# The front state's turn between its two gate steps: VectorE block transposes and sixteen on-chip transfers instead of eight TensorE transposes, with the loop in another order

## The reference, cut to what matters

```
layer 0, three steps:  a  = adj @ h                        (per graph)
                       z  = sigmoid(a.W3 + h.U3 + b)       r = sigmoid(a.W4 + h.U3 + b)
                       hv = tanh(a.W5 + (r*h).U5 + b)      h = (1-z)*h + z*hv
layer 1: q,k,v from x;  rel = adj.T * (q @ k.T), each row divided by its norm;  rel @ v
layer 2: (adj @ x) @ W + b          layer 3: (normalised adj) @ (x @ W) + b
```

## Time and profile before

| | |
|---|---|
| median of three runs | 1271.95 us |
| the profiled execution | 1271.8 us |
| its span, first to last instruction | 1270.0 us |
| mean granted TensorE clock | 0.995 of full |
| TensorE busy / VectorE / ScalarE / GpSimd | 98% / 81% / 46% / 15% |
| one turn of the loop | 76.5 us |

### The profile page before, as it was taken

One profiled execution on the slowest core, in us unless ns is written; L12 is line 12 of the kernel. 1 busy time (PEld: TensorE's weight loads), 2 busy tenths in 40 slices (PEclk: granted clock), 3 DMA queues, 4 the chain that ended last, 5 costly groups with the idle time before them and its releaser, 6 DMA issues.

```text
span 1270.0 us, 21112 instructions
## 1 busy us (share of the span) xinstructions
PE 1240.6 (98%) x7664; PEld 1103.3 (87%) x7664; DVE 1031.4 (81%) x2274; ACT 583.7 (46%) x1007; POOL 192.4 (15%) x366
## 2 busy tenths in 40 slices
PE   7799999999999999999999999999999999999996
PEld 6589899898988989899898988989889898998895
DVE  5668889788888878888788888878888788895898
ACT  4444444444444444454444444444454445444442
POOL 0001112020210202112020110202112021110023
PEclk9999999999999999999999999999999999999999
DMA  7020110202001020010202002020010202000000
GB/s 199 1 50 1 38 30 1 66 0 59 7 17 50 0 66 0 33 33 0 66 0 50 17 17 50 0 66 0 21 45 0 66 0 49 17 17 18 1 1 34
DMA packets 86168, 37.56 MB, mean 30 GB/s; under 512 B 64768, under 2 KB 83200, under 8 KB 86144
## 3 DMA queue, kind: packets, MB, share of 16 engines
q1 hardware_dynamic: 84592, 36.71, 10.6%
q0 software_dynamic: 192, 0.52, 0.2%
q10 hardware_dynamic: 1360, 0.01, 0.1%
HBM read 20.45 MB, written 8.39 MB: 23 GB/s over the span
## 4 chain that ended last, share of the span: by engine, by line
PE 94%; DVE 4%; DMA 1%; POOL 1%; issue 0%; ACT 0%; ACTq 0%; DVEq 0%
PE b_ps L430 46%; PE f_ps L430 43%; PE f_ps L525 2%; PE b_ps L525 1%; DMA bias_in<-in_L_gnn_u_b 1%; PE b_ps L571 1%; DVE f_stats L1251 0%; DVE hf_feat L1267 0%; DVE normed L1267 0%; POOL f_rstd L364 0%; DVE f_cand L1184 0%; DVE b_stats L1251 0%; DVE f_kept L1178 0%; ACTq L827 0%; DVE f_a_lo L1162 0%
## 5 line engine op out<-in xcount | busy, mean ns | idle before, releaser
L362 POOL TENSOR_TENSOR b_var_eps<-b_moments,eps 128x2 f32<-128x2 f32 x120 | 44.1, 368 | 827.6 <-DVE b_moments L1258 827.6
L364 POOL TENSOR_TENSOR b_rstd<-b_var_eps,neg_half 128x2 f32<-128x2 f32 x120 | 97.0, 808 | 9.4
L866 ACT ACTIVATE f_z<-f_ps,bias_z 128x512 f32<-128x512 f32 x66 | 45.2, 685 | 92.5 <-PE f_ps L430 92.5
L870 ACT ACTIVATE f_cand<-f_ps,bias_c 128x512 f32<-128x512 f32 x66 | 45.5, 690 | 85.1 <-PE f_ps L430 85.1
L1168 DVE TENSOR_TENSOR f_gate<-f_gate,hf_feat 128x512 f32<-128x512 f32 x66 | 45.2, 685 | 46.2 <-ACT f_gate L858 46.0
L1251 DVE BATCH_NORM_STATS2 b_stats<-b_ps 128x6 f32<-128x256 f32 x180 | 68.3, 421 | 13.9 <-PE b_ps L430 13.3
L430 PE MATMUL f_ps<-adjT_hi,hf_node_hi 128*128 128x256 f32 x264 | 74.6, 283 | 0.0
L430 PE MATMUL f_ps<-adjT_hi,hf_node_lo 128*128 128x256 f32 x264 | 74.3, 282 | 0.0
L430 PE MATMUL f_ps<-adjT_lo,hf_node_hi 128*128 128x256 f32 x264 | 74.2, 281 | 0.0
L1290 DVE TENSOR_TENSOR b_rh_lo<-b_ps,b_rh_hi 128x512 fp32r<-128x512 f32 x90 | 61.9, 688 | 13.7 <-ACT b_rh_hi L824 13.4
L824 ACT ACTIVATE f_a_hi<-f_ps 128x512 fp32r<-128x512 f32 x66 | 39.0, 593 | 71.8 <-PE f_ps L430 71.8
(11 more groups left out here) (325 smaller groups left out, 4610.5 us busy)
## 6 DMA issues: line engine op xcount, KB each, us to landing
x_front<-in_x SPq DMA_DIRECT2D x16, 512.0 KB, 3.5
x_blocks<-in_x SPq DMA_DIRECT2D x60, 128.0 KB, 3.4
input_t<-hf_feat SPq DMA_DIRECT2D x15, 512.0 KB, 2.9
out<-result SPq DMA_DIRECT2D x15, 512.0 KB, 3.0
b_cand<-in_L_gnn_u_w SPq DMA_DIRECT2D x2, 256.0 KB, 8.9
bias_out<-in_L_gnn_bias POOLq DMA_DIRECT2D x4, 128.0 KB, 6.3
b_z<-in_L_gnn_w_w SPq DMA_DIRECT2D x1, 512.0 KB, 11.4
b_gate<-in_L_gnn_w_w SPq DMA_DIRECT2D x1, 512.0 KB, 12.4
```

The costliest lines, as they stand in the source:

```text
L364: pool.tensor_tensor(Y.rstd[:, g], Y.var_eps[:, g], neg_half[:], ALU.pow).then_inc(Y.s_rstd, 1)
L866: act.activation(L.z[:, k], L.ps0[:, k], ACT.Sigmoid, bias=bias_z[:, k:k + 1]).then_inc(L.s_z, 1)
L870: act.activation(L.cand[:, k], L.ps1[:, k], ACT.Tanh, bias=bias_c[:, k:k + 1]).then_inc(L.s_tanh, 1)
```

## The change

Only the turn of the front state inside the 14 bodies is done in another way; the prologue, the `finish` part and the back state keep `turn_h`. Two VectorE block transposes (`turn_state`) write each 32x32 block, turned in itself, to `blocks`, which lies over `front.gate`. SyncE then sends sixteen transfers of 32 partitions by 256 elements (32 KB each), which put the blocks on their right partitions in `moved`, over `front.z`. ScalarE and VectorE make `node_hi` and `node_lo` from there (`moved_hi`, `moved_lo`), once all sixteen have landed.

```diff
+        state_f.blocks, state_f.moved = quarters(front.gate), quarters(front.z)
 (SyncE)
+            def move_blocks(S, turn):
+                sp.wait_ge(S.s_blocks, 2 * turn)
+                for a in range(4):
+                    for b in range(4):
+                        sp.dma_start(S.moved[32 * a:32 * a + 32, b],
+                                     S.blocks[32 * b:32 * b + 32, a]).then_inc(S.s_moved, 16)
                 keep_input(p)
+                move_blocks(state_f, p)
                 store(main, p - 1)
 (ScalarE)
+            def moved_hi(S, v, g, turn):
+                act.wait_ge(S.s_moved, 256 * turn)
+                ...
+                rows = S.moved[:, :, g * P:(g + 1) * P].rearrange("p q (u i) -> p u q i", i=32)
+                copy(S.node_hi[:, g].rearrange("p h (c q i) -> p (h c) q i", q=4, i=32), rows).then_inc(S.s_node_hi, 1)
 (VectorE)
+            def turn_state(S, v, c):
+                dve.wait_ge(S.s_feat, upto(v, c))
+                out = S.blocks.rearrange("p q (u c i) -> p u q c i", c=C, i=32)[:, :, :, c]
+                dve.transpose(out, S.feat[:, c].rearrange("p (u q i) -> p u q i", q=4, i=32)).then_inc(S.s_blocks, 1)
+            def moved_lo(S, v, g):
+                dve.wait_ge(S.s_node_hi, upto(v, g))
+                ...
+                dve.tensor_tensor(cells(S.node_lo), rows, full(cells(S.node_hi)), ALU.subtract).then_inc(S.s_node_lo, 1)
```

All hand-written orders change with it. TensorE's body, in its middle part, is now:

```diff
                 candidate_reset(front, 2 * p, 1)
+                for k in range(2):
+                    keys(main, q, k)
                 values(main, q, 0)
+                relate(main, q, 0)
+                values(main, q, 1)
                 relate(main, q, 1)
-                for k in range(2):
-                    turn_h(state_f, 2 * p + 1, k)
-                values(main, q, 1)
+                base(front, 2 * p + 1, 0)
                 sum_squares(main, q, 0)
                 attend(main, q, 0)
-                mix(front, 2 * p + 1, 0)
+                base(front, 2 * p + 1, 1)
+                for k in range(2):
+                    mix(front, 2 * p + 1, k)
                 sum_squares(main, q, 1)
                 attend(main, q, 1)
-                mix(front, 2 * p + 1, 1)
-                for k in range(2):
-                    base(front, 2 * p + 1, k)
                 reset(front, 2 * p + 1, 0)
```

More of the change, by code:

```diff
@@ L686, in finish @@
                     turn_h(state_f, 2 * LAST + 1, k)
-                candidate_mixed(back, LAST - 1, 0)
-                update(back, LAST - 1, 0)
+                for k in range(2):
+                    update(back, LAST - 1, k)
                 for k in range(2):
@@ L706, in finish @@
                 candidate_reset(back, LAST - 1, 1)
-                base(front, 2 * LAST + 2, 0)
                 for k in range(2):
                     mix(front, 2 * LAST + 2, k)
+                base(front, 2 * LAST + 2, 0)
+                turn_sum(main, LAST - 1, 0)
+                reset(front, 2 * LAST + 2, 0)
+                keys(main, LAST - 1, 0)
                 base(front, 2 * LAST + 2, 1)
[L711 to L714, removed]
+                reset(front, 2 * LAST + 2, 1)
                 update(front, 2 * LAST + 2, 0)
+                turn_sum(main, LAST - 1, 1)
+                update(front, 2 * LAST + 2, 1)
+                relate(main, LAST - 1, 0)
                 candidate_mixed(front, 2 * LAST + 2, 0)
-                update(front, 2 * LAST + 2, 1)
-                keys(main, LAST - 1, 0)
                 candidate_reset(front, 2 * LAST + 2, 0)
@@ L928, in body @@
+                sum_hi(main, q, 1)
                 for k in range(2):
[L929 to L939, removed]
@@ L940, in body @@
-                update_gate(front, 2 * p, 0)
-                rh_hi(front, 2 * p, 1)
+                    rh_hi(front, 2 * p, k)
+                for k in range(2):
+                    update_gate(front, 2 * p, k)
+                for k in range(2):
+                    candidate(front, 2 * p, k)
                 keys_hi(main, q, 0)
-                candidate(front, 2 * p, 0)
+                feat_hi(state_f, 2 * p + 1, 0)
+                keys_hi(main, q, 1)
+                values_hi(main, q, 0)
@@ L953, in body @@
                 relation_hi(main, q, 1)
+                for k in range(2):
+                    moved_hi(state_f, 2 * p + 1, k, p)
                 relation_squares(main, q, 1)
-                values_hi(main, q, 1)
-                feat_hi(state_f, 2 * p + 1, 1)
                 for k in range(2):
                     a_hi(front, 2 * p + 1, k)
-                for k in range(2):
-                    conv_x_hi(main, q, 0, k)
+                conv_x_hi(main, q, 0, 0)
+                reset_gate(front, 2 * p + 1, 0)
@@ L1026, in finish @@
-                for k in range(2):
-                    sum_hi(main, LAST - 1, k)
-                for k in range(2):
-                    reset_gate(front, 2 * LAST + 2, k)
+                feat_hi(state_f, 2 * LAST + 2, 0)
+                node_hi(state_f, 2 * LAST + 2, 0, 5)
+                candidate(back, LAST - 1, 0)
+                node_hi(state_f, 2 * LAST + 2, 1, 6)
+                feat_hi(state_f, 2 * LAST + 2, 1)
+                candidate(back, LAST - 1, 1)
+                a_hi(front, 2 * LAST + 2, 0)
@@ L1030, in finish @@
+                sum_hi(main, LAST - 1, 0)
+                a_hi(front, 2 * LAST + 2, 1)
+                sum_hi(main, LAST - 1, 1)
+                reset_gate(front, 2 * LAST + 2, 0)
+                keys_hi(main, LAST - 1, 0)
+                rh_hi(front, 2 * LAST + 2, 0)
+                reset_gate(front, 2 * LAST + 2, 1)
                 update_gate(front, 2 * LAST + 2, 0)
-                for k in range(2):
-                    rh_hi(front, 2 * LAST + 2, k)
+                rh_hi(front, 2 * LAST + 2, 1)
@@ L1042, in finish @@
[L1042 to L1050 removed]
+                sum_hi(last_pair, 0, 0)
+                values_hi(main, LAST - 1, 0)
@@ L1343, in body @@
+                rh_lo(back, q, 0)
+                reset_h(back, q, 1)
                 turn_blocks(p, 1)
+                a_lo(front, 2 * p, 0)
+                rh_lo(back, q, 1)
                 keep(back, q, 1)
+                input_lo(p, 1)
+                a_lo(front, 2 * p, 1)
+                residual(main, back, q, q, 1)
                 candidate_part(back, q, 0)
-                input_lo(p, 1)
                 new_sum(main, q, q, 0)
-                for k in range(2):
-                    a_lo(front, 2 * p, k)
@@ L1370, in body @@
+                normalise(main, q, 0, 0)
+                keep(front, 2 * p, 1)
+                moments_of(main, q, 0, 1)
+                sum_lo(main, q, 1)
+                candidate_part(front, 2 * p, 0)
+                first_h(p, 0)
+                turn_state(state_f, 2 * p + 1, 0)
+                candidate_part(front, 2 * p, 1)
+                first_h(p, 1)
+                turn_state(state_f, 2 * p + 1, 1)
+                keys_lo(main, q, 0)
                 normalise(main, q, 0, 1)
```

468 lines of the change are left out of this document (227 added, 241 removed).

## The result

The changed kernel takes 1329.71 us (median of 4 runs), the kernel before 1272.86 us beside it: a ratio of 1.044 [1.042, 1.046]. So it is slower, as forecast, but by 57 us and not by 17, and 5 us beyond the upper end of the range. The profiled execution took 1329.41 us, its span is 1327.3 us. One of the four runs took 1349.07 us, at a mean clock of 0.961 where the other three had 0.982 to 0.985; there is no trace of it.

A forecast was written before the change was run, and what follows sets the result against it. TensorE, never waiting in the 14 bodies, was taken as the bound. Each body waits 2.1 us and saves 0.87: 14 x (2.1 - 0.87) = +17.2 us on 1271.8, so 1289.0; range 1262 to 1325.

The forecast's parts named there:

- step 3: Sixteen sends in SyncE's one queue: 0.54 us from one start to the next, the last starting at T+11.5.
- the new order: Changed order of engine work at the start of the loop body and on GpSimd: costed at nothing.
- Removed turn: Front state's transposes on TensorE taken out of 14 loop bodies: 0.87 us a body, 12.2 us gained in all.
- Steps 1 and 2: New front state on ScalarE and VectorE done at T+2.43, then its second block transpose done at T+3.3.
- T: Moment in a loop body at which TensorE goes on from candidate_reset(front, 2p, 1); the new chain is timed from it.
- Step 4: Landing of a 32 KB send: 1.7 us after issue, upper bound 2.9; the last lands at T+13.2.
- Step 5: High and low parts on ScalarE and VectorE before `mix`: 2.0 us, so `mix` can start at T+15.2.
- the cover: TensorE's work before `mix`, nine calls and `sum_squares`: 13.1 us, leaving a wait of 2.1 us in each body.
- rival B: Sends as dear as `x_blocks`, spacing 0.64 us, wait 3.6 us, and TensorE's clock falls: 1310 us or 1327; chance 20%.
- clock term: TensorE's clock at half behind each wait: up to 2.4 us a body, up to +34 us; with half of it, 1327.

## Why the prediction was wrong in size

The direction, the place and the chain behind the wait were right. What failed is step 3, the spacing of the sends, which made each wait too short, and the loss of clock behind the waits, which was left out of the sum. Of the 40 us that were missed, the length of the waits has 20, the clock 15 and the new order 3; the slow step behind each wait (14 x 0.11) and the smaller gain make up the rest.

- **Removed turn**, 12.2 us: measured 11.4 (the run without transfers against the new order with the old turn). Right.
- **Steps 1 and 2**, transposes done at T+3.3: measured 588.44 + 0.71 = 589.15, T+3.18. The strided writing costs nothing (0.71 us against 0.70). Right.
- **Step 3, the spacing of the sends**: 0.54 forecast, 0.633 measured. This is the first of the two that failed. I had taken the 512 KB copy's 0.54, taken 0.06 off for its wait, and put 0.06 on as the distance to a neighbour. But the first send, which carries a wait, is the shortest here (579 ns, the others 591): the 0.06 for a wait, read from the `x_blocks`, isn't there. The send itself takes 0.591 us where 0.48 was forecast, the distance to the next 0.042 where 0.06 was. 15 x 0.09 = 1.4 us; less the 0.06 forecast for the wait and the 0.1 by which the sends start earlier, it puts the last send at T+12.7 instead of T+11.5. The row that would have said it was the one for 32 partitions, `x_blocks` with 0.58, which I had as the upper bound: 0.58 + 0.06 = 0.64. Not for its partitions, as the run over 128 partitions shows. Why a copy of 512 KB between the same kinds of memory takes 0.54 and these take 0.59 stays open; bytes (16 or 32 KB) and partitions (32 or 128) are not the reason.
- **Step 4, the landing**: 1.7 forecast, 1.9 measured. Taking 512 KB's time down to 32 KB's share was nearly right.
- **Step 5 and the cover**: 2.0 us from the copies' start to `mix` (600.58 to 602.58) and a cover of 13.1 us (13.19): both right. So the wait is T+16.6 less T+13.2, 3.4 us where 2.1 was forecast, and 14 times 1.3 is 18 us. The two first bodies of the loop wait for 4.15 and 4.31 us, with sends up to 1.64 us long: 2 us more.
- **The clock**: 14.9 us, measured by keeping TensorE busy. The forecast left it out of the sum, since the one wait of 2.59 us seen had no fall behind it, and priced it in rival B at half of a possible 34 us. That is near, but by a guess: it halved 14 losses of 2.4 us, and what came were eight falls, most at 1.6 us. Reading one wait of 2.59 as "this length is safe" was the error, and the changed kernel has that very wait, at the same place before the loop, with a fall behind it. Its line and the stretch behind it (granted clock 0.50), then the same stretch in the kernel before (1.00):

```profile
36.71 1.09 PE L540 MATMUL f_ps<-ident,hf_feat 128*128 128x128 f32 x8 [2.58 <-DVE hf_feat L1210]
...
37.72:41.12 3.40, 3.10 (x8) 2.44 (x8) 3.32 (x7) 1.75 (x4) 0.00 (x0) 0.50 0.00 0
...
37.83:41.23 3.40, 3.10 (x14) 2.46 (x14) 3.34 (x7) 1.77 (x4) 0.00 (x0) 1.00 0.00 0
```

Elsewhere 2.0 us was enough in some bodies, and of waits of 3.2 and 3.3 us one kernel lost it in all bodies and the other in about every second. The Trainium skill, "TensorE: Matmul & The Clock Gate", Part 1, gives 1.2 GHz as the state of an idle TensorE; the trace agrees, since each fall in the loop begins in a wait or within 1.6 us of its end. A term for it belongs in any sum that adds a wait to a TensorE that had none.

- **The new order**, costed at nothing: 2.8 us by the medians of the runs, 0.27 us a turn and 3.7 us in 14 turns by the two profiles.

Together, in the spans of the profiled executions, one kernel after the other: 1270.0 us before; 1275.0 with the new order (+5.0, of which the fall at 37 us, which comes and goes, has 1 to 2); 1263.6 with the old turn gone and nothing to wait for (-11.4); 1312.6 with the sends and their waits, TensorE kept busy (+49.0); 1327.3 with the clock falling too (+14.7). That is rival B with its clock term (3.6 us of wait, 1327 us), which had been given 20%. The forecast's range ended at 1325, below this rival's own 1327, so its upper end didn't follow from its working.

The Trainium skill, "DMA: Bandwidth & Descriptors", Anatomy of one DMA, gives the sequencer's dispatch about 50 ns, for transfers from GpSimd's queue and as one part of their fixed time. In the two-queue run a send held GpSimd's queue for 0.496 us in all, ten times that, so the 50 ns are no price for a send; sends on SyncE's queue, 0.591 us here, are not what that section is about. The Rules for kernel authors of the same page of the Trainium skill have a sentence that did come true, and that the forecast didn't use: that spreading transfers over several engines saves sequencers' time for issuing, while it brings no bandwidth. The two-queue run is just that, 5.0 us side by side instead of 10.1 in a row.

## What to carry to other kernels

Count small transfers by their number in a queue, not by their bytes: in a chain that something waits for, each costs the whole distance from one issue to the next (0.63 us on SyncE here), and the nearest row for that distance is that of another short send in the same queue, bounds included. Before giving such a change up, put the sends on a second queue: 5 us less on the chain turned a loss of 57 us into a gain of 9. And where TensorE has never waited in a loop, a new wait of 2 us or more can cost more than its length, so price the clock in the sum; by how much depends on where the waits fall, and a change that shortens one a little can make it worse.

## What the runs showed of the hardware that was not expected

- **The wait of a send added nothing to its price, its bytes made no difference, and its shape little.** 579 ns for the first with its wait, 591 for the others, with 16 KB or 32 KB alike; 528 and 601 over 128 partitions. Other kinds of send do differ (0.39 to 0.58 us in the earlier trace rows). GpSimd's queue was quicker than SyncE's with the same transfers (line 396 against line 345; eight in 3.98 us against 5.02):

```profile
L396 POOL DMA_DIRECT2D f_z<-f_gate x112: 496/496/552, 103.7 to 1091.2; - x112
...
L345 SPq DMA_DIRECT2D f_z<-f_gate x112: 579/591/1754, 103.5 to 1092.0; - x112
```

- **The clock can fall behind quite short waits, and a small shift decides how often.** In the 14 bodies of each profile: with waits of 0.92 us none (and one behind a wait of 1.84 in the same run); with 2.00 us, two; with 3.27 us, eight (seven of 3.4 us, one of 6.8); with 3.36 us, eleven (seven of 3.4 us, four of 6.8); with 3.18 us, fourteen (twelve of 6.8 us, two of 3.4); none where matmuls that nobody needs filled the wait. Why the pattern comes out one way or the other was not settled.
- **The first sends of the loop are slow** (up to 1.64 us against 0.59, one slow send in each of the first two bodies). These bodies wait 4.2 and 4.3 us in place of 3.3. No run asked for the reason.
